# Vision tower on one core: embedding spread over the attention of the image group before, narrower Gram products, evictions moved between ScalarE and VectorE

## What is computed

```python
h = patches @ W + b                                            # 4096 tokens x 256
n = layernorm(h); q, k, v = split(n @ qkv_w.T + qkv_b)         # 16 heads of 16
keep = top_k(sigmoid(sigmoid(relu(n @ r_w1.T + r_b1) @ r_w2.T + r_b2)), 25 of 64 keys)
h = h + softmax(where(keep, q k.T / 4, -1e30)) @ v             # within each image
n = layernorm(h); h = h + silu(n @ sw1.T) * (n @ sw3.T) @ sw2.T + routed(n)   # 8 experts, top 2
n = layernorm(h); h = h + (polymax(causal(q k.T / 4)) @ v) @ W_proj
n = layernorm(h) / (rms + 1e-8); g = gelu(n @ ternary(w_up).T)
h = h + (g / (rms(g) + 1e-8)) @ ternary(w_down).T
```

## Time and profile before

| | before |
|---|---|
| median of 3 runs | 913.06 us (912.74 to 914.14) |
| profiled execution | 912.48 us, its span 910.7 us |
| busy, share of the span | PE 85%, VectorE 70%, weight loads 60%, ScalarE 46%, GpSimd 8% |
| granted TensorE clock, mean | 0.924 |
| seven repetitions of the first half's loop | 57.4 to 400.7 us |
| eight blocks of the second half and its tail | 480 to 910.7 us |

### The profile page before, as it was taken

The page is one execution under the profiler, slowest core; times in us unless marked ns, Lnnn a source line. Parts: engine busy times, 40 slices in busy tenths (PEclk is TensorE's granted clock), DMA queues, the critical chain, the costliest instruction groups (busy, mean ns, idle before and its releaser), DMA issues.

```text
span 910.7 us, 23464 instructions
## 1 busy us (share of the span) xinstructions
PE 770.1 (85%) x9831; PEld 545.5 (60%) x9831; DVE 640.8 (70%) x1443; ACT 419.9 (46%) x600; POOL 71.2 (8%) x62
## 2 busy tenths in 40 slices
PE   2769898999989898976796889898989989898966
PEld 2446665757575656655384567575866756575734
DVE  6467878777777878777598286867959676483742
ACT  3333534353535343442233563937466491745521
POOL 0000000010101010000002010000101000010000
PEclk9979999999999999995875989999999999998968
DMA  8060010101010100200000000000000000000000
GB/s 308 2 229 2 9 62 0 69 0 69 0 69 0 69 0 0 92 1 1 1 1 1 2 1 26 0 23 0 7 16 0 23 1 24 1 24 2 2 23 24
DMA packets 6779, 26.97 MB, mean 30 GB/s; under 512 B 2256, under 2 KB 3152, under 8 KB 5072
## 3 DMA queue, kind: packets, MB, share of 16 engines
q1 hardware_dynamic: 6736, 26.35, 7.8%
HBM read 22.15 MB, written 4.19 MB: 29 GB/s over the span
## 4 chain that ended last, share of the span: by engine, by line
PE 39%; issue 33%; DVE 17%; ACT 7%; POOL 2%; DMA 1%; DVEq 0%; POOLq 0%; SPq 0%; ACTq 0%
PE PS L335 8%; PE PS L695 5%; PE PS L660 3%; PE PS L637 3%; PE PS L346 2%; PE PS L325 2%; PE PS L683 2%; PE PS L673 2%; PE PS L554 2%; PE PS L631 2%; PE PS L651 2%; PE PS L307 2%; ACT w_s L955 1%; PE PS L438 1%; DVE wup_s L1468 1%
## 5 line engine op out<-in xcount | busy, mean ns | idle before, releaser
L673 PE MATMUL PS<-xT,wqkv_h 128*128 128x512 f16 x256 | 70.8, 431 | 23.9 <-ACT w_s L955 22.1
L307 PE MATMUL PS<-tokW_h,w_s 128*128 128x256 f16 x576 | 67.7, 278 | 16.3 <-DVE w_s L1311 16.3
L830 ACT ACTIVATE Pm<-Pm 128x1024 f32<-128x1024 f32 x32 | 33.9, 1058 | 83.7 <-DVE Pm L1237 83.7
L307 PEld LDWEIGHTS PS<-tokW_h,w_s 128*128 128x128 f16 x576 | 56.8, 100 | 24.1 <-issue 16.3
L1573 DVE TENSOR_TENSOR work<-w_s,work 128x512 f16<-128x512 f32 x48 | 32.5, 689 | 47.5 <-ACT work L957 47.5
L837 ACT ACTIVATE PT<-PS 128x512 f32<-128x512 f32 x64 | 37.5, 596 | 59.8 <-PE PS L428 59.8
L1030 POOL TENSOR_TENSOR rstd<-ve,mhalf 128x4 f32<-128x4 f32 x24 | 28.0, 1168 | 470.1 <-DVE ve L1146 470.1
L673 PEld LDWEIGHTS PS<-xT,wqkv_h 128*128 128x128 f16 x256 | 25.1, 107 | 64.5 <-ACT w_s L955 32.4
L325 PE MATMUL PS<-ident_s,xn 128*128 128x128 f32 x256 | 45.6, 302 | 15.5 <-DVE xn L1150 14.9
L335 PE MATMUL PS<-xT,wat_h 128*128 128x512 f16 x192 | 48.3, 414 | 7.6 <-DVE xT L1509 7.6
L695 PE MATMUL PS<-tokW_h,work 128*128 128x256 f16 x448 | 51.3, 273 | 0.5 <-DVE msq L1580 0.5
(11 more groups left out here) (243 smaller groups left out, 1643.8 us busy)
## 6 DMA issues: line engine op xcount, KB each, us to landing
work<-in_x SPq DMA_DIRECT2D x8, 1536.0 KB, 6.4
out<-H SPq DMA_DIRECT2D x8, 512.0 KB, 2.6
w_s<-in_w SPq DMA_DIRECT2D x3, 1024.0 KB, 6.9
wup_s<-in_wup SPq DMA_DIRECT2D x1, 1024.0 KB, 5.3
wdn_s<-in_wdn SPq DMA_DIRECT2D x1, 1024.0 KB, 7.3
w_s<-in_tokW SPq DMA_DIRECT2D x1, 768.0 KB, 7.5
wup_s<-in_wqkv SPq DMA_DIRECT2D x1, 768.0 KB, 8.1
wdn_s<-in_s SPq DMA_DIRECT2D x3, 256.0 KB, 6.0
```

Source lines behind the costliest of these rows:

```text
L307: m = pe.matmul(dst, halves_[xi][:, k, rows], w[:, wi, k, cols], start=(n == 0), stop=(n == 3 * chunks - 1))
L673: m = pe.matmul(PS[:, UP_BANKS[f % 4], :], wup_h[:, c, f * P:(f + 1) * P], part[:, c, :], start=(k == 0), stop=(k == 2 * C - 1))
```

## The change

- The embedding of a group goes in four pieces: tile 0 at the end of the repetition before, tile 1 behind the transposes of tile 1, tile 2 behind it, tile 3 behind the values of tile 1. It uses banks 7 and 4. The patches are split one repetition earlier: ScalarE behind the copies of x1, VectorE in two pieces around `slot_in`.
- VectorE takes `soft` of tiles 2 and 3 ahead of `attend(0)`, and statistics and normalization by pairs of tiles; GpSimd raises each pair to its power alone.
- The softmax tiles 2 and 3 are turned in banks 0 to 3; turning tile 2 waits for both `soft`.
- Both key chunks and the high half of the shared expert's hidden state go to ScalarE.
- Second half: the Gram product takes blocks of 32 columns by 64, four side by side, into bank 6 alone; half of them (f - 4) run inside `B3_up`, which has three banks instead of four. Gelu and the copy of its high half are interleaved with the chunk before. The squares of tiles 0 and 1 go to VectorE (`v_quads`). `B3_down` of tiles 0 and 1 no longer waits for the sums of squares. The routed sums are computed turned round, so that a transpose and a copy at the end fall away. In `B3_down_last` the wait for all Gelus falls away.

```diff
-        UP_BANKS = (4, 6, 7, 5)
-        GRAM_LAG = NF
+        UP_BANKS = (4, 7, 5)
+        GRAM_LAG = 4
+        TURN_BANKS = ((4, 5), (4, 5), (0, 1), (2, 3))
@@ PE, first half
                 if half == 0:
                     pe.wait_ge(p_exp, TILES * g + t + 1)
-                if t % 2:
-                    pe.wait_ge(pt_out, 2 * (TILES * g + t) + half - 1)
+                    if t == 2:
+                        pe.wait_ge(p_sub, TILES * g + TILES)
+                if t == 1:
+                    pe.wait_ge(pt_out, 2 * TILES * g + half + 1)
...
                 if nxt:
+                    embed(g + 1, (1,))
                     pe.wait_ge(pt_out, 2 * (TILES * g + 1) + 1)
-                    embed(g + 1, (0,))
+                    embed(g + 1, (2,))
+                    pe.wait_ge(embed_out, 2 * g + 3)
                 values(g, 1, 0)
                 values(g, 1, 1)
                 if nxt:
-                    embed(g + 1, (1, 2, 3))
-                    pe.wait_ge(embed_out, 2 * g + 3)
+                    embed(g + 1, (3,))
...
                 weights_T(g, 2, 0)
-                if not isinstance(g, int):
-                    pe.wait_ge(embed_out, 2 * g + 4)
                 weights_T(g, 2, 1)
...
                 weights_T(g, 3, 1)
-                pe.wait_ge(pt_out, 2 * (TILES * g + 3) + 1)
                 turn(0)
...
                 A4(i, False)
+                if more:
+                    embed(i + 2, (0,))
@@ PE, second half
                 for k in range(RB):
-                    m = pe.matmul(PS[0:64, 2, 0:HID], one_hot_w[:, k, :], wz_k[:, k, :],
+                    m = pe.matmul(PS[:, 2, 0:64], wz_k[:, k, :], one_hot_w[:, k, :],
...
-                    if f >= 4:
-                        pe.wait_ge(g_ok, NF * g + f - 3)
+                    if f >= 3:
+                        pe.wait_ge(g_ok, NF * g + f - 2)
...
                 pe.wait_ge(gl_out, NF * g + f + 1)
                 for t in range(TILES):
-                    m = pe.matmul(PS[:, 6 + t // 2, (t % 2) * E:(t % 2 + 1) * E], G_hi[:, f, t * P:(t + 1) * P],
-                                  G_both[:, f, :, t * P:(t + 1) * P], start=(f == 0 and t % 2 == 0),
-                                  stop=(f == NF - 1), skip_group_check=True)
+                    for i in range(4):
+                        at = t * P + 32 * i
+                        m = pe.matmul(PS[32 * i:32 * i + 32, 6, t * 64:(t + 1) * 64], G_hi[:, f, at:at + 32],
+                                      G_both[:, f, :, at:at + 32], start=(f == 0 and t == 0), stop=(f == NF - 1),
+                                      tile_position=(0, 32 * i), skip_group_check=True)
...
-                    if t % 2 == 0:
-                        pe.wait_ge(msq_ok, TILES * g + t + 2)
+                    if t == 2:
+                        pe.wait_ge(msq_ok, TILES * g + TILES)
@@ ScalarE
+            def keys(g, c):
+                act.wait_ge(k_mm, 2 * g + c + 1)
+                for e in range(2):
+                    act.activation(kM[:, c, e, :], PS[:, c, :], ACT.Identity, bias=bkp[:, c, e:e + 1],
+                                   scale=par_s[:, e:e + 1]).then_inc(k_out, 1)
...
+                for c in range(C):
+                    act.wait_ge(hs_ok, 2 * g + c + 1)
+                    act.activation(hs_hi[:, c, :], hs[:, c * TOK:(c + 1) * TOK], ACT.Copy).then_inc(hs_high, 1)
...
-                    act.activation(g32[f], PS[:, UP_BANKS[f % 4], :], ACT.Gelu).then_inc(g_ok, 1)
-                    act.wait_ge(g_ok, NF * g + f + 1)
-                    act.activation(G_hi[:, f, :], g32[f], ACT.Copy).then_inc(gh_out, 1)
+                    act.activation(g32[f], PS[:, UP_BANKS[f % 3], :], ACT.Gelu).then_inc(g_ok, 1)
                     if f < 2 and nxt:
-                        quads(g + 1, f)
                         lins(g + 1, f)
+                    if f > 0:
+                        g_high(g, f - 1)
+                g_high(g, NF - 1)
@@ VectorE
+            def slot_A(i, more):
+                soft(i, 2)
+                soft(i, 3)
                 attend(i, 0)
-                soft(i, 2)
+                embed_h(i + 1, 0)
+                stats1(i + 1, 0)
                 attend(i, 1)
-                soft(i, 3)
-                embed_h(i + 1)
-                norm1(i + 1)
+                embed_h(i + 1, 1)
+                stats1(i + 1, 1)
+                norm1(i + 1, 0)
+                norm1(i + 1, 1)
                 attend(i, 2)
                 attend(i, 3)
                 x1_low(i + 1)
                 stats2(i)
-                slot_in(i + 1, lambda: norm2(i), lambda: x2_low(i))
+                norm2(i)
+                if more:
+                    low_patches(i + 2, (0,))
+                slot_in(i + 1, last_x4=lambda: x2_low(i))
+                if more:
+                    low_patches(i + 2, (1,))
                 v_A4(i)
...
+            def v_quads(g, t):
+                dve.wait_ge(relu_ok, TILES * g + t + 1)
+                v = relu_s[t % 2][:, :]
+                dve.tensor_tensor(v, v, v, ALU.mult).then_inc(quadv_ok, 1)
```

More of the change, by code:

```diff
@@ L357, in A2 @@
                 proj_T(4, rW1_h, 0, (x1_hi, x1_lo), h1_mm, 64)
-                if not first(g):
-                    pe.wait_ge(p_sub, TILES * g)
                 for c in range(C):
@@ L519, in _ @@
             scores(0, 0)
-            with pe.Fori(0, LAST) as i:
+            embed(1, (0,))
+            def slot_A(i, more):
                 scores(i, 1)
@@ L537, in routed_tables @@
                     m.then_inc(tab_mm, 1)
-                for n in range(2):
-                    pe.wait_ge(tabT_ok, n + 1)
-                    pe.transpose(PS[0:64, 4 + 2 * n, 0:P], AC[n][:, :], ident_s[:, :]).then_inc(tab_t, 1)
+                pe.wait_ge(tabT_ok, 1)
+                pe.transpose(PS[0:64, 4, 0:P], AC[0][:, :], ident_s[:, :]).then_inc(tab_t, 1)
             def routed_count():
@@ L600, in B1_qk @@
                         pe.wait_ge(h5_ok, TILES * (g - 2) + 2 * c + 2)
-                    elif not first(g) and c == 1:
+                    elif not first(g) and c == 0:
                         pe.wait_ge(h4_ok, 1)
-                    proj_T(6 + c, wat_h, c * P, (x1_hi, x1_lo), Bq_mm)
+                    proj_T(7 - c, wat_h, c * P, (x1_hi, x1_lo), Bq_mm)
             def B1_v(g, tiles):
@@ L813, in a_A2 @@
                 act.activation(t2[:, :], sg1[:, :], ACT.Tanh, scale=0.5).then_inc(rt2, 1)
[L814 to L817 removed]
+                keys(g, 1)
                 last_x4()
@@ L1306, in _, with low_patches @@
             low_weights(0, 1)
-            def low_patches(g):
-                for k in range(2):
+            def low_patches(g, parts=range(2)):
+                for k in parts:
                     ks = slice(k * KP // 2, (k + 1) * KP // 2)
@@ L1315, in _ @@
             low_weights(1, 7)
-            embed_h(0)
-            norm1(0)
+            for p in range(2):
+                embed_h(0, p)
+                stats1(0, p)
+            for p in range(2):
+                norm1(0, p)
             x1_low(0)
@@ L1340, in _ @@
                 v_shared(i)
+            with dve.Fori(0, LAST - 1) as i:
+                slot_A(i, True)
+            slot_A(LAST - 1, False)
             def each(v):
```

172 lines of the change are left out of this document (91 added, 81 removed).

## The result

| | before | after |
|---|---|---|
| median | 913.45 us (4 runs, 912.74 to 914.14) | 853.71 us (4 runs, 852.98 to 854.66) |
| profiled execution, span | 912.48, 910.7 | 853.78, 851.9 |
| granted clock, mean | 0.924 | 0.948 |

The ratio is 0.9347 (95% interval 0.933 to 0.9363). The sign is as forecast, and so are most of the milestones inside a repetition and a block; the size is not, and part of the way in which the second half gains is not either.

What follows compares the result with a forecast made beforehand. It took PE work plus the gaps in it as the bound. Savings of 23.8 - 2.0 + 15.0 + 2.8 + 4.1 = 43.7 us turned the profiled 912.48 into 868.8, forecast as 869, range 857 to 887.

Steps and rivals of the forecast that it cites:

- a rival (861, 15%): First half: no half-clock stretches and the full chain, 7 x 3.9 + 4 us instead of 23.8, giving 861; chance 15%.
- the first half: Seven repetitions: each 45.0 us, 3.4 less, together 23.8 us saved; the chain alone gave 44.5.
- the six blocks: Second half, blocks 1 to 6: 2.5 us less each, 15.0 us together.
- Tile 0: First half: its 2.05 us of embedding products move into the PE's 2.2 us gap, a repetition ahead.
- Keys and hidden halves: First half: evictions and casts move to ScalarE; the 0.5 us wait for the hidden state's last half shrinks to about 0.15.
- The rival that only tile 0 pays: First half: VectorE's long order runs late, so 14.4 us is saved instead of 23.8, time 878; chance 15%.
- Behind the loop: Ahead of and behind the first half's loop: 2.0 us lost together.
- The squares in block 0: First block: two squarings move to VectorE, which is the chain there, costing 2.4 us.
- ScalarE's saving goes nowhere: Second-half blocks: ScalarE ends 2.5 us earlier, but VectorE is late next, its chain ending at 15.6 us, before 16.0.
- The Gram's price: Second half: narrow Gram products, four side by side, at 17 ns each, taken from the values row; bounds 14 and 116 ns.
- The slower rival (from 75 ns): Second half: narrow Gram products don't run side by side; at 116 ns each, time 955; chance 3%.
- Block 7 and tail: End of the second half: block 7 saves 2.8 us of VectorE's Gram wait, the tail 4.1 us.

Runs made afterwards that it cites:

- e4: Changed kernel with tile 0 of the embedding back in its own repetition, reopening the PE gap ahead of the scores of tiles 2 and 3; 875.82 us.
- e5: Changed kernel with tile 0 back in its own repetition and the reopened gap filled with 18 products nobody reads; 870.60 us.
- e6: Changed kernel with the narrow Gram products all behind the next scores, none inside the up product; 864.70 us.
- e12: Changed kernel with narrow Gram products all behind the next scores, and 15 unread products filling the PE's waits for VectorE's last low halves; 855.19 us.
- e1: Kernel before the change, with 18 unread products filling the 2.2 us PE gap ahead of the scores of tiles 2 and 3 in each repetition; 912.70 us.
- e3: Changed kernel with the squares of tiles 0 and 1 of the next scores back on ScalarE; 870.79 us.
- e7: Changed kernel with the first key chunk's evictions and the two high halves of the hidden state back on VectorE; 863.90 us.
- e2: Changed kernel with the earlier wide Gram product, all behind the next scores, four up-product banks and the down product's old waits; 875.85 us.
- e13: Changed kernel with the copy of each Gelu's high half right behind that Gelu again, for all Gelus; 850.89 us.
- e15: Changed kernel with unread products in its long waits and the copies of the first two Gelus right behind them, other six interleaved; 839.26 us.

## Why the prediction was wrong

**The step that failed is the price of a PE gap.** My sum charged an idle gap its own length and wrote "half-clock stretches cost some 4 us beside 7 x 48.4" off as a rival (861, 15%), for the first half alone; for the second half I did not look at the clock at all. The runs show that such stretches follow from the gaps (e4 against e5, e6 against e12), so a change that closes a gap can get back more than the gap. In the sum the terms that came out too small by it are the first half (23.8 forecast, 30.4 measured) and the six blocks (15.0 and 21.0), 12.6 of the 15 us together. How much of that is the clock is known in part: 2.6 us in the third and seventh repetitions, which e1 gets back by filling the gap alone; 2.0 in the first, less the 0.8 by which it starts later, where a stretch moved ahead of the loop; up to 4.3 in the blocks, which is a remainder, as the kernel before was never run with the waits of its blocks filled. The rest of the 15 us has other causes, below. The rows that warned of it stood in my own windows: 0.95 beside 1.00 for the same instructions.

**First half, 3.4 us per repetition: measured 3.63.** Tile 0 gave 1.97 (2.05 forecast). Keys and hidden halves I gave 0.35 us through the wait for the last half; undoing them costs 1.13. 0.5 is left for softmax order and banks, if the parts add up, which wasn't tried. The chain had given 44.5, and I raised it to 45.0 by adding small waits to "the PE's own work 44.2". The measured 44.76 lies half way between the two. Waits are 1.3 us and PE busy time is 43.35, against the 44.2 that I held for work. The rival that only tile 0 pays is refuted.

**Behind the loop, 2.0 lost: measured 0.6.** The squares in block 0 cost about what I said (2.6 in e3, 2.4 forecast). More can't be said, as the same code took 117.1 to 119.4 us there from one execution to the next; whether the halves give more than the 0.85 I took stays open (e7 loses 1.2 to 3.5 there, keys included).

**Blocks, 2.5 us: measured 2.8 at full clock.** Milestones were hit to 0.15 us. What they were put down to was wrong. "ScalarE's saving goes nowhere" is false: with the squares on ScalarE the block takes 51.60 instead of 49.61. The table of full-clock blocks is not additive:

| | squares on ScalarE | squares on VectorE |
|---|---|---|
| wide Gram, late | 52.39 (before) | 52.10 (e2) |
| narrow Gram in the up loop | 51.60 (e3) | 49.61 (after) |

All but the first have ScalarE's new order, too, and that order costs 1.1 us in the last of them (48.51 without it, e13). Without the squares' move the rest gives 0.8, without the Gram it gives 0.3; together it is 2.8. The last low half lay at 15.6, where I had it, so the right number came in part by luck, out of a chain in which I took VectorE's start for fixed; it is set by ScalarE's first copies (e3, e13, e15).

**The Gram's price** was right in kind: 11 ns a product where I took 17 from values. The slower rival (from 75 ns) is refuted. For the routed sums, 3.68/32 = 115 ns a record against 116 before: streaming half the columns brought nothing. By the Trainium skill (TensorE: Matmul & The Clock Gate, LDWEIGHTS; TensorEngine Tiling, Restrictions) a load of 32 columns would be 27 ns, as an estimate. The trace does not agree, as I had assumed: 64 products with their loads take 0.73 us. The same rule's 107 ns for 128 columns is near the 115 of the routed sums.

**Block 7 and tail**, 6.9 forecast, 8.9 measured: I have not taken the 2.0 apart. The granted clock of block 7 is 0.80 before and 0.85 after, of the tail 0.83 and 0.84, so part of it may be the clock again; that was not tried.

## What to carry to other kernels

Before summing what a change removes, compare the granted clock of stretches with the same instructions: where it differs, look for a PE gap ahead of the slow one, and give each gap that closes a second price (here 1.2 to 2.4 us for one of 2.5 in the profiled execution, 0.9 by the medians). A gap that can't be closed with work can be filled with products that nobody reads, and this is also the quickest experiment: it keeps all work and takes away the idle time alone. In a chain over three engines, what counts is when the pacing engine gets its first operand, not how many microseconds the feeding engine saves in all.

## What the runs showed of the hardware that I had not expected

- A PE gap of 2.51 us was followed by half clock in each of six repetitions of e4, while one of 2.18 to 2.19 us in the kernel before was in only two of six, and 0.55 in none. In e6 waits of 0.88 in the up loop and 1.11, 0.30, 0.30 and 0.30 us behind the scores came before it in every block from the second on; e12 keeps the 0.88 and stays at full clock.
- The same waits don't always have the same effect. In the blocks of the kernel before the PE waits 1.19 and 1.97 us in the up product, with four products between; half clock followed in four of five such blocks. The changed kernel's 1.11 and 1.61 us were followed by it in no block.
- The trigger need not be a wait. From 435.0 to 462.5 us the changed kernel is at half clock, and the PE is busy without a break in the microseconds ahead: it runs the f32 products of the experts' tables, 8 columns each, from 431.66 us on. That these products are the cause was not tried.

```profile
431.66 10.65 PE L542 MATMUL PS<-x,w_s 128*128 128x8 f32 x64
```

- Four side by side, f16 products of 32 columns by 64 cost 11 ns each, loads included, less than the 17 ns per record of the like f32 values, of which each product has two.
